# A gated recurrence of six layers on one core: the first loads put into one stream in order of need, and the table gathers put into another order

## The reference

```
def _L0_rec_ref(state, token, ih, hh):     # state 2048 x 256, token 2048, ih 6 x 4000 x 256, hh 6 x 256 x 256
    for i in range(n_layers):              # 6
        gate = ih[i][token]
        state = jnp.tanh(state + jnp.matmul(state, hh[i]) * gate)
    return state
```

## Time and profile before

| | |
|---|---|
| median of 3 runs | 105.76 us (105.54, 105.76, 106.26) |
| the profiled execution | 106.02 us |
| its span in the trace | 104.2 us, mean granted clock 0.948 |
| busy shares | PE 84%, DVE 76%, ACT 70%, POOL 63% |
| read from HBM, written | 19.14 MB, 2.10 MB |
| gathers: packets, bytes | 2304, 3.71 MB |

### The profile page before, as it was taken

The page is one execution under the profiler, slowest core; times in us unless marked ns, Lnnn a source line. Parts: engine busy times, 40 slices in busy tenths (PEclk is TensorE's granted clock), DMA queues, the critical chain, the costliest instruction groups (busy, mean ns, idle before and its releaser), DMA issues.

```text
span 104.2 us, 1794 instructions
## 1 busy us (share of the span) xinstructions
PE 87.1 (84%) x650; PEld 74.4 (71%) x650; DVE 79.2 (76%) x127; ACT 73.5 (70%) x129; POOL 65.7 (63%) x60
## 2 busy tenths in 40 slices
PE   5919909895498998987999989999899998999900
PEld 5817608474386896976898978999789897898800
DVE  2179085283979399996979879798897978989990
ACT  4078020891897818799799996999969999667431
POOL 2687787734043008694897939979398893992440
PEclk9995885589999999999999999999999999999998
DMA  3899999999699915542387523555319654095355
GB/s 39 285 367 401 417 388 376 315 307 347 205 215 268 188 36 101 104 79 48 75 58 145 97 60 58 101 101 101 72 29 86 121 101 94 18 130 221 147 201 201
DMA packets 27128, 17.46 MB, mean 168 GB/s; under 512 B 22421, under 2 KB 22677, under 8 KB 27120
## 3 DMA queue, kind: packets, MB, share of 16 engines
q1 hardware_dynamic: 24816, 13.64, 55.2%
q0 software_dynamic: 2304, 3.71, 9.9%
HBM read 19.14 MB, written 2.10 MB: 204 GB/s over the span
## 4 chain that ended last, share of the span: by engine, by line
PE 51%; DMA 16%; DVE 13%; issue 9%; SPq 3%; ACT 3%; POOL 2%; POOLq 0%; DVEq 0%
PE products L278 38%; PE turned L310 7%; DMA state<-in_state_rows 6%; DVE sums L434 5%; DMA gates<-in_gate_rows,index 5%; PE products L270 5%; DMA w_full<-in_weights 5%; DVE sums L442 4%; ACT gates L336 1%; POOL sums L262 1%; DVE split_rows L455 1%; DVE split_cols L448 1%; ACT state L372 1%; SPq L190 1%; POOL gates L255 1%
## 5 line engine op out<-in xcount | busy, mean ns | idle before, releaser
L262 POOL TENSOR_TENSOR sums<-sums,state 128x512 f32<-128x512 f32 x37 | 46.8, 1274 | 21.4 <-DVE sums L434 20.5
L278 PE MATMUL products<-w_head,split_cols 128*128 128x256 f16 x316 | 54.8, 273 | 1.5 <-issue 1.5
L372 ACT ACTIVATE state<-sums 128x512 f32<-128x512 f32 (+1 forms) x49 | 30.2, 619 | 19.9 <-DVE sums L442 10.9
L278 PE MATMUL products<-w_rest,split_cols 128*128 128x256 f16 x158 | 43.1, 273 | 0.0
L278 PEld LDWEIGHTS products<-w_head,split_cols 128*128 128x128 f16 x316 | 30.9, 98 | 5.8 <-issue 2.3
L434 DVE SCALAR_TENSOR_TENSOR sums<-products,w_down,gates 128x512 f32<-128x512 f32 (+1 forms) x40 | 29.3, 735 | 0.3 <-PE products L278 0.2
L270 PE MATMUL products<-w_full,first_cols 128*128 128x256 f32 x64 | 20.1, 471 | 8.7 <-DMA first_cols<-in_state_cols 6.0
L270 PEld LDWEIGHTS products<-w_full,first_cols 128*128 128x128 f32 x64 | 14.5, 237 | 13.6 <-DMA first_cols<-in_state_cols 7.4
L255 POOL DMA_INDIRECT gates<-in_gate_rows,index x13 | 14.3, 1099 | 10.2 <-ACT gates L336 6.8
L278 PEld LDWEIGHTS products<-w_rest,split_cols 128*128 128x128 f16 x158 | 15.4, 98 | 1.7
L455 DVE SCALAR_TENSOR_TENSOR split_rows<-copies,split_rows 128x512 f16<-128x512 f32 x19 | 13.0, 686 | 3.9 <-ACT split_rows L360 3.7
(11 more groups left out here) (30 smaller groups left out, 28.5 us busy)
## 6 DMA issues: line engine op xcount, KB each, us to landing
first_cols<-in_state_cols SPq DMA_DIRECT2D x8, 256.0 KB, 5.0
state<-in_state_rows SPq DMA_DIRECT2D x8, 256.0 KB, 5.9
out<-state SPq DMA_DIRECT2D x7, 256.0 KB, 2.0
w_full<-in_weights SPq DMA_DIRECT2D x6, 256.0 KB, 5.2
last_row<-in_gate_rows SPq DMA_DIRECT2D x1, 768.0 KB, 4.6
split_cols<-split_rows SPq DMA_TRANSPOSE x19, 3.1
gates<-in_gate_rows,index POOLq DMA_INDIRECT x16, 5.5
out<-state SPq DMA_DIRECT2D x2, 128.0 KB, 1.9
```

What stands on the lines that cost most here:

```text
L262: nc.gpsimd.tensor_tensor(sums[:, q], sums[:, q], pair_rows(state, q), ALU.add).then_inc(pool_added, 1)
L278: last = nc.tensor.matmul(bank[:, j, :], split_cols[:, q, s, j, k, :], w[:, l - 1, k * HID:(k + 1) * HID], start=(n == 0), stop=(n == len( ...
L372: nc.scalar.activation(pair_rows(state, q)[:, cut], sums[:, q, cut], ACT.Tanh).then_inc(state_ready, 1)
```

## The change

- All loads of layer 0's columns, the rows and the weights stand ahead of SP's loop, in one written order: columns 2, rows 0, weights 1, columns 3, rows 1, and so on to rows 7. Each one waits for the landing of the load four places ahead of it, so that four are under way. No load waits for a product any more.
- SP's loop holds only the transposing DMAs, with no lag (`LOAD_LAG` is gone).
- `WHOLE` is (14, 15): these two tiles are gathered whole and are issued first. Tiles 0 to 13 are filled and gathered in part, in order.
- Fills: DVE 0, 2, 4, 6 ahead of step 0, then 8 and 10 after step 0 and 12 after step 1; ACT 1, 3, 5, 7 ahead, then 9, 11, 13 after steps 0, 1, 2.
- In the last layer the add of pair 6 goes from POOL to DVE.
- The weight preparation is one step later in places: sums of layers 2 to 5 at steps 3 to 6 (were 2 to 5), the first head at 4 (3), the first rest at 5 (4), the second totals at 10 (9), later heads and rests one step later each.

```
-    LAST_ON_DVE = (3, 5, 7)
-    WHOLE = 3
-    ACT_FILLS = {-1: (4, 7, 10), 1: (12,), 3: (14,)}
-    DVE_FILLS = {-1: (3, 5, 6, 8, 9), 0: (11,), 2: (13,), 3: (15,)}
+    LAST_ON_DVE = (3, 5, 6, 7)
+    WHOLE = (14, 15)
+    ACT_FILLS = {-1: (1, 3, 5, 7), 0: (9,), 1: (11,), 2: (13,)}
+    DVE_FILLS = {-1: (0, 2, 4, 6), 0: (8, 10), 1: (12,)}
-    SUMS_AT = {0: 0, 2: 1, 3: 2, 4: 3, 5: 4}
-    TOTALS_AT = {3: 0, 9: 1}
-    HEADS_AT = {3: 0, 12: 1, 20: 2, 28: 3, 36: 4}
-    RESTS_AT = {4: 0, 13: 1, 21: 2, 29: 3, 37: 4}
+    SUMS_AT = {0: 0, 3: 1, 4: 2, 5: 3, 6: 4}
+    TOTALS_AT = {3: 0, 10: 1}
+    HEADS_AT = {4: 0, 13: 1, 21: 2, 29: 3, 37: 4}
+    RESTS_AT = {5: 0, 14: 1, 22: 2, 30: 3, 38: 4}
-    LOAD_LAG = 3
             load_cols(0)
             load_weights(0)
             load_cols(1)
+            sp.wait_ge(last_in, 16)
+            load_cols(2)
+            sp.wait_ge(cols_in[0], 16)
             load_rows(0)
+            sp.wait_ge(w_in[0], 16)
+            load_weights(1)
+            sp.wait_ge(cols_in[1], 16)
+            load_cols(3)
+            sp.wait_ge(cols_in[2], 16)
+            load_rows(1)
+            sp.wait_ge(rows_in[0], 16)
+            load_cols(4)
...
+            sp.wait_ge(rows_in[4], 16)
+            load_weights(5)
+            sp.wait_ge(w_in[4], 16)
+            load_rows(6)
+            sp.wait_ge(cols_in[7], 16)
+            load_rows(7)
+
             for i in range(STEPS):
-                if i + 2 < PAIRS:
-                    sp.wait_ge(product_ready, i + 1)
-                    load_cols(i + 2)
-                    load_rows(i + 1)
...
-                if i >= LOAD_LAG and by_dma(i - LOAD_LAG):
-                    q = order[i - LOAD_LAG][1]
-                    sp.wait_ge(rest_rows_ready, dma_turns(i - LOAD_LAG))
+                if by_dma(i):
+                    q = order[i][1]
+                    sp.wait_ge(rest_rows_ready, dma_turns(i))
+            for t in WHOLE:
+                pool.indirect_dma_start(row(t), None, gate_rows, offset(t)).then_inc(gates_in[t // PAIR], 16)
             for t in range(TILES):
-                if t < WHOLE:
-                    pool.indirect_dma_start(row, None, gate_rows, offset).then_inc(gates_in[t // PAIR], 16)
+                if t in WHOLE:
                     continue
```

More of the change, by code:

```diff
@@ L203, in _ @@
             load_cols(1)
+            sp.wait_ge(last_in, 16)
+            load_cols(2)
+            sp.wait_ge(cols_in[0], 16)
             load_rows(0)
-            for i in range(STEPS):
-                if i + 2 < PAIRS:
-                    sp.wait_ge(product_ready, i + 1)
-                    load_cols(i + 2)
-                    load_rows(i + 1)
[L210 to L216, removed]
-                if i >= LOAD_LAG and by_dma(i - LOAD_LAG):
-                    q = order[i - LOAD_LAG][1]
-                    sp.wait_ge(rest_rows_ready, dma_turns(i - LOAD_LAG))
+            sp.wait_ge(w_in[0], 16)
[6 more added lines that the diff above has]
+            load_cols(4)
+            sp.wait_ge(w_in[1], 16)
+            load_rows(2)
+            sp.wait_ge(cols_in[3], 16)
+            load_weights(2)
+            sp.wait_ge(rows_in[1], 16)
+            load_cols(5)
+            sp.wait_ge(cols_in[4], 16)
+            load_rows(3)
+            sp.wait_ge(rows_in[2], 16)
+            load_weights(3)
+            sp.wait_ge(w_in[2], 16)
+            load_cols(6)
+            sp.wait_ge(cols_in[5], 16)
+            load_rows(4)
+            sp.wait_ge(rows_in[3], 16)
+            load_weights(4)
+            sp.wait_ge(w_in[3], 16)
+            load_cols(7)
+            sp.wait_ge(cols_in[6], 16)
+            load_rows(5)
+            sp.wait_ge(rows_in[4], 16)
[4 more added lines that the diff above has]
+            load_rows(7)
+            for i in range(STEPS):
+                if by_dma(i):
+                    q = order[i][1]
+                    sp.wait_ge(rest_rows_ready, dma_turns(i))
                     sp.dma_start_transpose(split_cols[:, q].rearrange("p s j k r -> p (s j k) r"),
@@ L244, in _, with offset, row @@
             by_vector = [t for tiles in DVE_FILLS.values() for t in tiles]
+            def offset(t):
+                return bass.IndirectOffsetOnAxis(ap=index[:, t:t + 1], axis=0)
+            def row(t):
+                return gates[:, t].rearrange("p l h -> p (l h)")
+            for t in WHOLE:
+                pool.indirect_dma_start(row(t), None, gate_rows, offset(t)).then_inc(gates_in[t // PAIR], 16)
             for t in range(TILES):
-                offset = bass.IndirectOffsetOnAxis(ap=index[:, t:t + 1], axis=0)
-                row = gates[:, t].rearrange("p l h -> p (l h)")
-                if t < WHOLE:
-                    pool.indirect_dma_start(row, None, gate_rows, offset).then_inc(gates_in[t // PAIR], 16)
+                if t in WHOLE:
                     continue
@@ L254, in _ @@
                     pool.wait_ge(vector_filled, by_vector.index(t) + 1)
-                pool.indirect_dma_start(row, None, gate_rows, offset, bounds_check=VOCAB - 1,
+                pool.indirect_dma_start(row(t), None, gate_rows, offset(t), bounds_check=VOCAB - 1,
                                         oob_is_err=False).then_inc(gates_in[t // PAIR], 16)
```

## The result

The changed kernel takes 108.62 us (median of 4 runs, 107.35 to 109.17); the kernel before takes 105.78 (4 runs, 105.54 to 106.26). The ratio is 1.022, interval 1.013 to 1.032. Timed again later, beside other kernels on one chip, it was 108.39 us and 1.029 (1.022 to 1.037). The forecast was 101.0: the change was to save 4.8 us and costs 2.8. The profiled execution took 109.17 us, with a span of 107.4; it is the slowest of the four.

What follows compares the result with a forecast made beforehand. Layer 0 was taken as bound by arrivals and late requests, later layers by PE. 106.02 - 4.7 (g(7) earlier) - 0.1 (tail) = 101.2 profiled, median 0.26 lower, 101.0; forecast band 100.2 to 102.0 (0.50), whole range 99.2 to 103.0.

Steps and rivals of the forecast that it cites:

- The step that failed: Weight preparation on ACT and DVE: steps beyond the first head and rest move one step later, at no cost.
- DVE and ACT in layer 0: Layer 0 work: DVE alone would reach g(7) at 28.6; g(6)'s gates limit, and ACT's fills come in time.
- nothing but PE's work counts: Later layers: PE is busy 12.45 of 12.74 us, so only its work counts, and the change leaves it alone.
- The ruler: From layer 0's end on: all that follows moves by as much as g(7), if engines bring no more backlog.
- g(7) itself: Last gating of layer 0, on DVE: starts at 32.0 (31.7 to 32.9) instead of 36.73, 4.7 us earlier.
- The loads: SP's layer 0 loads, four under way: 0.85 us each, columns 7 at 24, rows 7 at 27.5.
- slow bound: Other bound for SP's loads: 1.25 us each, columns 7 at 28 and rows 7 at 34.
- The tail: Kernel's end: pair 6's add moves from POOL to DVE and saves a collision; gain 0.1 us, bounds +0.6 and -0.8.
- PE in layer 0: Products 0, 1 and 2 follow each other without the 2.89 us idle; each later product is ready for its gating.
- C: Rival: after PE's idle, layer 0's products 2 to 7 run at 1.2 GHz; g(7) at 35.6, 104.6 us; chance 0.05.
- D: Rival: PE idles some 3 us before p(8), then 1.2 GHz slows layer 1's first products; 109.0 us; chance 0.04.
- lock between DVE and GpSimd: DVE copies locking POOL's gather issue: about 0.4 us of a 0.95 us copy taken; full lock would give 102.6.

Runs made afterwards that it cites:

- e2: Kernel before with only the weight heads and rests of layers 2 to 5 one step later, as in the changed kernel: 111.88 us beside 107.01.
- e1: Changed kernel with second totals and the weight heads and rests of layers 2 to 5 one step earlier, as before: 103.04 us, ratio 0.976.
- e5: e1 with tiles 0 and 1 gathered whole instead of 14 and 15, fills moved along: 101.26 us, ratio 0.948; timed again 102.57 us, 0.973.
- e11: The changed kernel timed again, unaltered, with a profiled execution of its own: 108.39 us, ratio 1.029.
- e3: Changed kernel with the last layer's add of pair 6 back on POOL: 108.95 us.
- e7: e1 with weights 1 and all loads behind it held until the gates of pair 0 are in: 104.35 us, ratio 0.976.
- e9: e5 with six loads under way instead of four: 103.43 us, ratio 0.979.

## Why the prediction was wrong

**The step that failed** is one sentence at the end of "DVE and ACT in layer 0": "The other weight steps move by one step with slack of several." I gave it no row and put its cost at nothing. Its price was 4.8 to 5.6 us (e2: 111.88 beside 107.01, and 109.84 beside 105.00; e1: 103.04, where the change has 108.39 and 108.62 in other sets), and 6.1 in both traces of the changed kernel, 1.7 of it the clock: more than the whole forecast gain. The rows that would have shown it were at hand: the kernel before shows a 0.28 us gap of PE at 61.7, 74.44 and 87.19, ahead of the first product of each later layer, and DVE's rest ends just there. A step that ends 0.1 us before it is needed has no slack. How much would be lost, 0.97 us per layer, those rows alone don't say. I had looked at these four table entries as four edits "with slack", while each acts once per layer, four times, and acts in the stage that I had myself named as the only one that counts in full: "nothing but PE's work counts, and the change doesn't touch it". It did touch it.

**The ruler** ("by how much g(7) moves, all that follows moves") holds with the tables of before: from the kernel before to e1, g(7) moves by 2.8 us and the span by 3.0; to e5, by 4.8 and 5.0. Between the two executions of the changed kernel it holds as well: 1.2 and 1.3.

**g(7) itself** was forecast at 32.0, between 31.7 and 32.9, and came at 34.03 and, in e11, at 32.80: 2.7 and 3.9 us gained, not 4.7. Only the first has the wait that I forecast (g(6) waits for its gather, g(7) doesn't). Two terms made the difference. Tile 0 was issued at 7.62, not 6.85, and tile 13 at 26.24, not 25.5 (7.94 and 26.11 in e11); and tile 13 took 5.9 us to land where I had sided with 4.4. In e11 it took 4.5, in e1 and e3 6.0: with the shorter landing my bounds hold, by the luck of the execution. Tile 0's issue lies 0.8 us behind the end of the fill that it waits for, in e1 and e11 as well. At the front, tile 1 landed at 15.4 instead of 13.3, of which 1.1 us is the loads beside it (e7). I had taken its landing as that of the queue ahead of it; its own was 6.3 us.

**The loads** came between my two bounds and nearer to the slow one: after the whole gathers a load took 3.7 to 5.4 us to land with four under way, about 1.1 us each instead of 0.85. Columns 7 landed at 26.9 (forecast 24, slow bound 28), rows 7 at 32.4 (27.5 and 34). Yet no add waited for rows in this trace. The first transposing DMA, behind them, took 5.9 us and p(9) began at 33.2, 1.6 us later than I had it, 0.9 of it waited for that DMA; g(9) was not due before. **The tail** gave 0.05 us, forecast 0.1 (e3). **PE in layer 0** had no idle time between products 0, 1 and 2, as said, but 1.54 us ahead of p(3), for the late g(0), and in e11 1.53 ahead of p(2), for columns 2. One reading of mine was off by a little: over both stretches up to 36.7 us PE is busy 73% of the time, not 74; nothing hangs on it.

**The rivals.** C looked for the low clock in layer 0's products and D at p(8), where it didn't come (from 13 to 36.7 us the clock is 1.00 in the changed kernel). It came at p(16), behind the 2.31 us gap that the late rest made. D's price of some 4 us and its sign were near the truth for a wrong reason; its cause was not the one that the runs showed. Of the lock between DVE and GpSimd (the Trainium skill, "SBUF — State Buffer", section "SBUF: two separate sides") the trace after has a larger case: in the issue at 17.14, beside two fills of DVE in a row (16.81 to 18.63), POOL took 1.61 us instead of 0.99. That is 0.6 us for 1.5 us of copies beside it, again less than the page's full block.

**What stays open.** Why tile 13's gather lands in 4.5 us in one execution and in 5.9 in another, and what holds tile 0's issue. Why tile 1's small gather still needs 5 us with the loads held back (e7). Why e5 timed 101.3 in one set and 102.6 in the other; the clocks differ, but what decides over them between executions of one program no run here shows. The 9.2 us landing in e9 lies beside more loads and the first transposing DMAs; which of the two did it wasn't tried, nor was a version that keeps the first transposing DMAs ahead of the last loads.

## What to carry to other kernels

Where a program is laid out by step numbers, a shift by one step in a loop body is a change of the steady state: count how often it acts, and price it by the gap ahead of its consumer, not by its distance in steps. A wait that ends 0.1 us before its consumer has no slack, even if its gap is only 0.28 us now. Give the expensive, early data to the consumer that comes first (the whole gathers to pair 0, e5), and let the paced list end on the last consumer. Before a moment in one trace is read to half a microsecond, look at it in a second execution of the same kernel: here g(7) moved by 1.2 us between two.

## What the runs showed of the hardware

The clock of PE falls behind a gap even between long busy stretches: 2.31 us idle after full-speed work, then 1.2 GHz for about 3.5 us, 1.7 us lost, in three executions alike (the changed kernel, e3, e11). A gap of 1.33 us at the later layers' starts was not followed by it (granted clock 1.00 over 61.99 to 74.73), nor was one of 1.77 us ahead of p(16) in e2 (clock 1.00 on both sides). More loads under way are not free for what comes behind them: with six, the first transposing DMA took 9.4 us to land and tile 15's gather 9.2, against 5.9 for that DMA and 4.4 to 6.3 for the small gathers in the changed kernel with four, and 5.9 and 5.7 for tile 15's gather in the two traces of e5's kernel. The same gather of the same kernel is not a fixed time either: tile 13's landed after 5.9 us in one execution and after 4.5 in another.
